# A recurrent attention and feed-forward block: one program block for four batches, masks behind the exp, stacks refilled by group

## The reference

```python
xn = layernorm(x)
q, k, v = xn @ Wq, xn @ Wk, xn @ Wv              # k, v repeated for two heads each
norm = |xn|;  mean = mean over tokens
score = 0.7 * norm + 0.3 * (-(xn . mean) / (norm * |mean| + 1e-6))
lm = top 337 tokens by score, dilated by 2       # landmarks
mask = (j <= i) & ((i - j < 128) | lm[j])
s = softmax(q k / 4 + where(mask, 0, -10000)) @ v @ Wo
g = silu(gelu(xn @ ternary(w1).T + b1) @ ternary(w2).T + b2)
out = x + s * g
```

## Time and profile before

| | |
|---|---|
| profiled execution | 737.96 us |
| its span, first to last instruction | 736.3 us |
| mean granted TensorE clock | 0.935 of 2.4 GHz |
| PE busy | 628.7 us, 85% |
| DVE busy | 375.4 us, 51% |
| ACT busy | 475.7 us, 65% |
| POOL busy | 74.7 us, 10% |
| scores, masks, values on PE (L718, L725, L738) | 198.5, 105.1, 167.4 us |
| exps on ACT (L812, L815) | 175.8, 204.9 us |

### The profile page before, as it was taken

The page is one execution under the profiler, slowest core; times in us unless marked ns, Lnnn a source line. Parts: engine busy times, 40 slices in busy tenths (PEclk is TensorE's granted clock), DMA queues, the critical chain, the costliest instruction groups (busy, mean ns, idle before and its releaser), DMA issues. The chain is left out here.

```text
span 736.3 us, 11753 instructions
## 1 busy us (share of the span) xinstructions
PE 628.7 (85%) x4336; PEld 351.7 (48%) x4336; DVE 375.4 (51%) x1002; ACT 475.7 (65%) x723; POOL 74.7 (10%) x92
## 2 busy tenths in 40 slices
PE   0537809999999989999999679999999899799982
PEld 0524604664455546654554536654554556334532
DVE  7968961665827434767454615648364521410101
ACT  1112417677877766697768556697768666888680
POOL 4000020020010201020100301110100210201001
PEclk9968957999999979999999869999999899899997
DMA  7000699000145659001190756001082691030101
GB/s 214 0 0 1 83 89 153 9 8 20 47 62 77 73 116 144 16 8 31 35 124 21 83 143 102 11 8 58 16 115 37 80 137 42 7 90 8 52 10 49
DMA packets 46833, 43.84 MB, mean 60 GB/s; under 512 B 6065, under 2 KB 41394, under 8 KB 46770
## 3 DMA queue, kind: packets, MB, share of 16 engines
q1 hardware_dynamic: 44642, 41.18, 33.6%
q10 hardware_dynamic: 2128, 1.84, 0.8%
HBM read 11.28 MB, written 4.19 MB: 21 GB/s over the span
## 5 line engine op out<-in xcount | busy, mean ns | idle before, releaser
L812 ACT ACTIVATE probs<-sc_ps,shift 128x512 f32<-128x512 f32 (+1 forms) x288 | 175.8, 617 | 102.0 <-PE sc_ps L725 101.3
L718 PE MATMUL sc_ps<-q_stack,k_stack 99*128 99x512 bf16 (+3 forms) x768 | 198.5, 344 | 33.3 <-PEq L189 14.7
L815 ACT ACTIVATE probs<-sc_ps,key_bias 128x1024 f32<-128x1024 f32 (+3 forms) x256 | 204.9, 818 | 16.5 <-PE sc_ps L718 15.8
L738 PE MATMUL att_ps<-probs,v_sb 128*32 128x512 f32 (+3 forms) x1536 | 167.4, 508 | 0.0
L718 PEld LDWEIGHTS sc_ps<-q_stack,k_stack 99*128 99x128 bf16 x768 | 50.2, 99 | 182.9 <-issue 70.8
L725 PE MATMUL sc_ps<-near_mask,mask_ident 128*128 128x256 bf16 (+1 forms) x576 | 105.1, 266 | 0.0
L850 POOL TENSOR_TENSOR h_lo<-hid,h_hi 128x512 fp32r<-128x512 f32 x32 | 43.2, 1350 | 342.3 <-DVE h_hi L882 342.3
L725 PEld LDWEIGHTS sc_ps<-near_mask,mask_ident 128*128 128x128 bf16 x576 | 56.4, 103 | 37.5 <-issue 7.1
L665 PE MATMUL aux_ps<-w2T,h_hi 128*128 128x256 f32 x256 | 70.1, 307 | 0.0
L665 PE MATMUL aux_ps<-w2T,h_lo 128*128 128x256 f32 x256 | 63.2, 279 | 0.0
L773 ACT ACTIVATE hid<-aux_ps,b_sb 128x512 f32<-128x512 f32 x64 | 42.9, 687 | 22.8 <-PE aux_ps L655 13.8
(11 more groups left out here) (152 smaller groups left out, 748.9 us busy)
## 6 DMA issues: line engine op xcount, KB each, us to landing
q_stack<-q_parts SPq DMA_DIRECT2D x96, 128.0 KB, 8.1
k_stack<-k_parts SPq DMA_DIRECT2D x24, 256.0 KB, 8.8
xn<-in_L_attn_hidden_states SPq DMA_DIRECT2D x4, 1024.0 KB, 8.2
attT<-att_raw SPq DMA_DIRECT2D x128, 32.0 KB
rden_bc<-den SPq DMA_DIRECT2D x64, 64.0 KB
probs<-in_L_ffn_w SPq DMA_DIRECT2D x2, 1024.0 KB, 7.8
out_y<-xn SPq DMA_DIRECT2D x4, 512.0 KB, 6.1
xn<-in_L_attn_hidden_states SPq DMA_DIRECT2D x3, 512.0 KB, 4.0
```

The lines of the kernel that those rows point to most:

```text
L718: last = pe.matmul(sc_ps[:, 2 * u + hh, lo:CH], k_stack[0:KROWS + SHIFT_ROWS, h // REP, kb * P:(kb + 1) * P], q_stack[0:KROWS + SHIFT_ROWS ...
L738: last = pe.matmul(att_ps[32 * q:32 * q + 32, n % 2, lo:CH], v_sb[:, kb, j * VW:j * VW + 32], probs[:, i % 3, q, lo:CH], start=(kb == 0), ...
L812: last = act.activation(probs[:, i % 3, us, lo:near], sc_ps[:, us, lo:near], ACT.Exp, bias=shift[:, 0:1], scale=HD ** -0.5)
L815: last = act.activation(probs[:, i % 3, us, near:CH], sc_ps[:, us, near:CH], ACT.Exp, bias=key_bias[:, kb:kb + 1], scale=HD ** -0.5)
```

## The change

The first blocks stay. Behind them the program now branches: the old turns are kept, for inputs with a large bound, as `general_path`, which these inputs do not take; the others take `fast_path`, a single block that is written out for all four batches (192 steps, numbered s; s % 48 is the old step number) with no barrier and no clearing between them. In it:

- **Masks.** `scores` has no mask matmuls and 96 rows in place of 99. `exps` makes one ACTIVATE for each u. Behind the exp POOL zeroes the upper triangle of the diagonal block (`causal`: a select on 128 x 4 x 128 numbers, in 32 steps of a batch), and DVE multiplies the next block by `near`, which is 1 within the window or for a landmark key (`local`: 128 x 4 x 128, in 28 steps). Queries beyond take `v_far`, a copy of V with the rows of all other keys zeroed, made once per batch in `commit`. So `values` of steps with both kinds (20 of a batch) have eight matmuls, on parts of the queries.
- **Values.** They are done for two steps together at each odd s, for s - 3 and s - 2, behind `scores(s, 1)`. At even s both halves of the scores stand together, ahead of the jobs; at odd s the jobs stand between the halves. `probs` has four buffers in place of three.
- **Stacks.** `q_stack` is a ring of three groups; each group has six DMAs of 64 KB (`fill_q`), issued when the group three before it has had its scores. `k_stack` is refilled for two key heads at a time (`fill_k`), when the last group that uses them is done. The columns of Wq and Wk are laid out by group for it.
- **Other.** The mean over tokens is summed on POOL (`token_sum`, seven additions of 128 x 256) and needs one matmul in place of eight. The squared norms of the tokens come from the layer norm's variance. x for the residual has a buffer of its own. The two clears of 32 rows of the stacks on DVE (L298, L299) are gone from the set-up. `ffn_up` of the next batch's chunk 0 stands at step 43.5 and `v_proj` at 42, where both came behind step 47. The table of the jobs' places has changed in small ways.

```diff
         exact = nc.values_load(exact_flag[0:1, 0:1], min_val=0, max_val=1)
-        turn(None, False, True, False, None)
-        turn(0, True, True, False, x[1])
-        with nc.Fori(1, B - 1) as b:
-            turn(b, True, True, True, x[b + 1])
-        turn(B - 1, True, False, True, None)
+        with nc.If(exact != 0):
+            general_path()
+        with nc.Else():
+            fast_path()
...
-                    def stack_q(c):
-
-                        cs = slice(c * CH, (c + 1) * CH)
-                        for i in range(NPART):
-                            for m in range(QT):
-                                sp.dma_start(q_stack[i * HD:(i + 1) * HD, m * HT:(m + 1) * HT, cs],
-                                             q_parts[:, m, QPART[i], cs]).then_inc(stack_in[c], 16)
...
+                        def fill_q(n):
+
+                            b, c, g = n // NG, n % NG // GROUPS, n % GROUPS
+                            m = g // QT
+                            if n >= QSLOTS:
+                                sp.wait_ge(sc_done, 2 * (GEND[n - QSLOTS] + 1))
+                            sp.wait_ge(q_split, QT * NC * b + QT * c + m + 1)
+                            for i in range(NPART):
+                                src = q_parts[half_rows(g), m, QPART[i], c * CH:(c + 1) * CH]
+                                sp.dma_start(q_stack[i * HD:(i + 1) * HD, n % QSLOTS, :, :], src).then_inc(q_in[n % QSLOTS], 16)
...
+                        def fill_k(b, g):
+                            if b:
+                                sp.wait_ge(sc_done, 2 * (GEND[(b - 1) * NG + GROUPS + g] + 1))
+                            sp.wait_ge(k_split, NC * (b + 1))
+                            for i in range(NPART):
+                                src = k_parts[g * 2 * HD:(g + 1) * 2 * HD, KPART[i], :]
+                                sp.dma_start(k_stack[i * HD:(i + 1) * HD, 2 * g:2 * g + 2, :], src).then_inc(k_in[g], 16)
...
-                                last = pe.matmul(sc_ps[:, 2 * u + hh, lo:near], mask_ident[:, :], near_mask[:, first:end:kb + 1, :],
-                                                 start=False, stop=True)
-                        last.then_inc(sc_done, 1)
...
+                        def exps(s, u):
+                            lo, _ = spans(s % NSTEP)
+                            if s >= NPROB and u == 0:
+                                act.wait_ge(pv_done, s - NPROB + 1)
                             us = slice(2 * u, 2 * u + 2)
-                            if near > lo:
-                                last = act.activation(probs[:, i % 3, us, lo:near], sc_ps[:, us, lo:near], ACT.Exp,
-                                                      bias=shift[:, 0:1], scale=HD ** -0.5)
-                            if near < CH:
-                                last = act.activation(probs[:, i % 3, us, near:CH], sc_ps[:, us, near:CH], ACT.Exp,
-                                                      bias=key_bias[:, kb:kb + 1], scale=HD ** -0.5)
-                            last.then_inc(exp_done, 1)
-
...
-                        lk(dve.tensor_scalar(near_mask[:, 0, :], before[:, :], MASK_UNIT, None, ALU.mult))
-                        for t in range(T - 1):
-                            last = dve.tensor_scalar(near_mask[:, t + 1, :], before[:, :], landmark[:, t:t + 1], -MASK_UNIT, ALU.max, ALU.mult)
-                        lk(last)
-                        dve.tensor_scalar(near_mask[:, 1:T, :], near_mask[:, 1:T, :], MASK_UNIT, None, ALU.add)
...
+                        def causal(s):
+                            c, _, kb = STEPS[s % NSTEP]
+                            own_q = slice((kb - TC * c) * P, (kb - TC * c + 1) * P)
+                            block_probs = probs[:, s % NPROB, :, own_q]
+                            pool.wait_ge(exp_done, 2 * (s + 1))
+                            pool.affine_select(out=block_probs, in_=block_probs, compare_op=ALU.is_ge, fill=0.0, base=0,
+                                               pattern=[[0, NQ], [1, P]], channel_multiplier=-1).then_inc(tri_done, 1)
...
+                        def commit(b):
+                            dve.wait_ge(v_done, 2 * (b + 1))
+                            if b:
+                                dve.wait_ge(pv_done, b * NSTEP - 2)
+                                dve.wait_ge(local_done, LOCALS[b * NSTEP - 1])
+                            for t in range(T - 1):
+                                dve.tensor_scalar(near[:, t, :], before[:, :], landmark[:, t:t + 1], None, ALU.max)
+                            dve.tensor_tensor(v_far[:, :, :], v_sb[:, b % 2], landmark[:, :].unsqueeze(2).to_broadcast([P, T, VP]),
+                                              ALU.mult).then_inc(far_done, 1)
+                            dve.wait_ge(far_done, b + 1)
+
+                        def local(s):
+                            c, _, kb = STEPS[s % NSTEP]
+                            nxt = slice((kb + 1 - TC * c) * P, (kb + 2 - TC * c) * P)
+                            block_probs = probs[:, s % NPROB, :, nxt]
+                            dve.wait_ge(exp_done, 2 * (s + 1))
+                            dve.tensor_tensor(block_probs, block_probs, near[:, kb, :].unsqueeze(1).to_broadcast([P, NQ, P]),
+                                              ALU.mult).then_inc(local_done, 1)
+
...
+                                pe.wait_ge(tri_done, TRIS[s])
+                            if has_local(s % NSTEP):
+                                pe.wait_ge(local_done, LOCALS[s])
+                            lo, end = spans(s % NSTEP)
+                            ends = [(v_sb[:, b % 2], lo, end), (v_far, end, CH)]
+                            for w, first, stop in ends:
+                                if first == stop:
+                                    continue
+                                for q in range(NQ):
+                                    j = (g * NQ + q) // REP
+                                    last = pe.matmul(att_ps[32 * q:32 * q + 32, n % 2, first:stop], w[:, kb, j * VW:j * VW + 32],
+                                                     probs[:, s % NPROB, q, first:stop], start=(kb == 0 and first == lo),
+                                                     stop=(kb == TC * (c + 1) - 1), skip_group_check=True)
...
-                                scores(i, 0)
-                            if i >= LAG:
-                                values(i - LAG)
-                            if i < NSTEP:
-                                scores(i, 1)
-                            for j in jobs_at(i, i + 0.5):
+                            if 0 <= s < TOTAL:
+                                scores(s, 0)
+                                if s % 2 == 0:
+                                    scores(s, 1)
...
+                            if 0 <= s < TOTAL and s % 2:
+                                scores(s, 1)
+                            if s % 2 and 3 <= s < TOTAL + 3:
+                                values(s - 3)
+                                values(s - 2)
...
+                        jobs += [(p + 16, "mean_row", b)]
+                        jobs += [(p + at, "transpose", b, n % KD, n // KD) for n, at in enumerate((19, 19, 20, 21))]
+                        jobs += [(p + 22 + c, "k_proj", b, c) for c in range(NC)]
+                        jobs += [(p + at, "q_proj", b, n % QT, n // QT) for n, at in enumerate((24, 26, 29, 31))]
+                        jobs += [(p + 30, "score_row", b, i) for i in range(2)]
+                        jobs += [(p + 41, "dilate", b)]
+                        jobs += [(p + 42, "v_proj", b, i) for i in range(2)]
+                        jobs += [(p + 43.5, "ffn_up", b, 0, f) for f in range(FT)]
...
+                    jobs += [(o + 10 + i, "ffn_down", b, i // 2, i % 2) for i in range(2 * TC)]
+                    jobs += [(o + 17.5, "ffn_up", b, 1, f) for f in range(FT)]
+                    jobs += [(o + 27 + t, "out_proj", b, t) for t in range(TC)]
+                    jobs += [(o + 34 + i, "ffn_down", b, TC + i // 2, i % 2) for i in range(2 * TC)]
+                    jobs += [(o + (57 + t // 2), "out_proj", b, TC + t) for t in range(TC)]
...
```

2108 lines of the change are left out of this document (1340 added, 768 removed).

## The result

The changed kernel takes 767.06 us (median of 4 runs, 765.11 to 773.68), the kernel before 737.26 in the same comparison: 1.0422 times as long, 95% interval 1.0351 to 1.0492. The forecast was 684, with a range of 656 to 718. It is slower by 30 us, where 54 us less were forecast.

What follows compares the result with a forecast made beforehand. PE's stream was taken as the bound in both chunks. 736.3 - 35.1 - 4.8 - 7.2 - 20.1 - 17.7 = 651.4; + 18 + 3 = 672.4; + 10 = 682.4, 684 us as device time; range 656 to 718.

Steps and rivals of the forecast that it cites:

- four chunks 0, with the boundary's wait: Chunk 0 of all four batches: 132.7 us against 167.8 before, plus 18 for waits at three boundaries.
- four chunks 1, with bursts and SILU: Chunk 1 of all batches: 322.9 us against 327.7; four bursts 7.2 less; boundary work 36.6 against 56.7.
- ranking 3, slip 10: Allowances: 3 us for products held back by DVE's bunched ranking, 10 us as 2% of 500 us.
- What is new on other engines: Select and product stay hidden, DVE has room for 28 products per batch; 3 us for ranking, 18 at boundaries.
- The boundary's wait: At each batch's step 9 PE waits 6 us at `out_proj` for heads behind DMAs; 3 x 6 = 18 us.
- Rival 2: PE's idle time in full pairs brings half clock, 2.7 us more per pair; chance 0.12, of which 0.08 slower.
- The pair order: A full pair of steps takes 5.19 us, PE's work only 3.57, leaving PE about 1.6 us idle for jobs.
- The split of the values: Values in two parts cost nothing more, the 0.15 counted once; otherwise 0.15 each on 80 steps, 12 us.
- Bursts: Four `ffn_up` bursts take 11 us instead of 12.8, as ACT starts its GELUs earlier: -7.2 us.
- The front: Set-up before the first exp: its place moves from 111.5 to about 93.8 us, -17.7; `lm_pad` about 94.
- mask matmuls cost PE in full: Mask matmuls on PE's stream: 6.2 us per batch in chunk 0, 7.0 in chunk 1, the latter mostly lost again.
- the detour's price of about nothing: Select on POOL and product on DVE, 1.6 us and two handovers, stay hidden within 2.7 us before the values.

Runs made afterwards that it cites:

- e13: Changed kernel with DVE's preparation jobs and chunk 0's `out_proj` at later places, `dilate` at step 46 behind the second burst: 746.9 us, 1.013 times the kernel before.
- e1: Changed kernel with the normalisation of chunk 0's heads at step 23 of DVE's list instead of 25: 757.1 us, 1.0305 times the kernel before.
- e9: Changed kernel with `out_proj` reading a tile of `xT_hi` instead of the normalised heads, attention left out of the output: 751.4 us, 1.0191 times the kernel before.
- e4: Changed kernel with 60 filler matmuls in front of the first `out_proj` of each chunk: 776.3 us, 1.0555 times the kernel before.
- e11: Changed kernel with DVE's preparation jobs and chunk 0's `out_proj` at later places, `dilate` at step 42: 772.4 us, 1.0471 times the kernel before.
- e10: Changed kernel without selects and products (masks missing), PE and ACT in the order of the kernel before: 735.1 us, 0.9973 times the kernel before.
- e7: Changed kernel without selects and products on the exp's results (masks missing), pair order kept: 757.1 us, 1.0274 times the kernel before.
- e2: Changed kernel with the single-step order of the kernel before on PE and ACT, masks kept: 785.2 us, 1.0642 times the kernel before.
- e8: Kernel before without the matmuls that add the masks to the scores: 696.4 us, 0.9438 times the kernel before.
- e6: Changed kernel with boundary list altered: x load behind the last sums, reciprocals, heads and layer norm later, all `out_proj` at step 58: 764.8 us, 1.0371 times before.
- e16: Changed kernel with e13's later places, single order with values of s - 3, and boundary reciprocals, heads and `out_proj` one step later: 733.3 us, 0.9961 times before.
- e17: e16 with the first batch's `dilate` at step 2 of PE's list instead of 0, near masks and two products behind it: 736.8 us, 0.9992 times before.

## Why the prediction was wrong

The terms, as the exps' starts give them, against the forecast (span 763.1 against 682.4, 80.7 us):

| term | forecast | measured | error |
|---|---|---|---|
| first exp's place | 93.8 | 92.9 | -0.9 |
| four chunks 0, with the boundary's wait | 150.7 | 175.0 | +24 |
| four chunks 1, with bursts and SILU | 403.5 | 473.3 | +70 |
| tail, as before | 21.4 | 21.9 | +0.5 |
| ranking 3, slip 10 | 13 | within the others | -13 |

**The step that failed** is "What is new on other engines", in the sentence on DVE's load: "That is room enough on the whole". It judged DVE by its busy share (58% now), with 3 us for the ranking. But PE doesn't wait for DVE's total; it waits for a certain place in DVE's list. I looked for such a meeting only at the boundary (step 9, 6 us), where the list was behind a DMA. The same meeting at step 27, where nothing but DVE's own work of steps 22 to 24 stood ahead, I did not look for: there 3 x 8.8 = 26 us. The experiments show it: the same operations at other places, 20 us less (e13); the wait taken from one job goes in part to the next in the list (e1, e9). These 26 us are a third of the 80.7. The other terms follow, of which the bursts weigh as much.

**The boundary's wait** had the right place and mechanism, and the wrong price. PE waited there 2.1 us for a product and 1.9 for the heads in batch 1, 2.5 and 2.4 in batch 2, and not at all in batch 3. The product stood behind the reciprocal, for which DVE waited:

```profile
275.73 0.94 DVE L1684 RECIPROCAL f_den<-f_den 64x128 f32<-64x128 f32 x1 [7.59 <-DMA f_den<-f_att_raw]
```

Steps 6 to 11 of batch 1 exceed the forecast's 13.6 without a wait by 11.0 us. The 7 beside the two waits go with the granted clock of 0.79; no run parts them further. The chain of DMAs itself was priced well: `den` landed 13.4 us after step 48's first exp (262.3; forecast 13.5), and L1689 ran at 283.65, 21.4 after it (forecast 22.5). But PE reached `out_proj` only 20.9 us after it, not 17.5, since it had lost time at the product before.

**The clock.** Rival 2 had half clock in the idle time of each full pair, for whole stretches. In chunk 1 that did not happen: steps 22 to 33 of batch 3, most of them without jobs, ran at 1.00. In chunk 0 it did happen in part. Steps 0 to 5 of batch 1 ran at 1.00 (the first row of the nine above), the same steps of batch 3 at 0.70, though no wait of PE in them was longer than 0.84 us. Here are these steps 0 to 5, then steps 22 to 33, of batch 3:

```profile
606.02:620.99 14.97, 11.69 (x90) 4.47 (x88) 7.85 (x14) 9.59 (x13) 5.69 (x6) 0.70 0.29 83
677.50:704.40 26.90, 22.55 (x201) 9.91 (x200) 8.46 (x12) 20.51 (x24) 9.46 (x10) 1.00 0.12 40
```

The same work took 3.3 us more. Why one batch and not the other, no run shows. The longer waits are plainer: from the first `dilate` to the last exp PE waited sixteen times for 1.88 us or more, and each time the granted clock fell to 1.2 GHz during the wait or within about 1 us of its end. That cost 3.5 us at step 27 (e4) and some 6 at `dilate` (e11). My slip of 2% has it far too small. Beside this stands the Trainium skill (TensorE: Matmul & The Clock Gate, "A second HAM failure mode: psum-queue depth-cycling"), which puts such falls down to short idle times between groups of matmuls; steps 0 to 5 of batch 3 fit that, those of batch 1, with waits up to 1.12 us, do not, and the costly falls here come with single waits of 2 to 10 us.

**The pair order** was priced right: 20/21 takes 4.95 us (5.10 forecast), 24/25 4.48 (4.13), 32/33 4.21 (4.13). What I had not seen is what it buys: a longer way from the exp to the values. I had it as a cost alone. It costs 22 us (e10 against e7), and while the product stands in DVE's list it saves that and 18 more (e2).

**The split of the values** priced at nothing is right. At full clock, the parts of steps 8 and 9:

```profile
296.29 0.64 PE L1392 MATMUL att_ps<-f_probs,f_v_sb 128*32 128x256 f32 x8
296.75 0.62 PE L1392 MATMUL att_ps<-f_probs,f_v_far 128*32 128x256 f32 x8
297.18 0.61 PE L1392 MATMUL att_ps<-f_probs,f_v_sb 128*32 128x256 f32 x8
297.61 0.40 PE L1392 MATMUL att_ps<-f_probs,f_v_far 128*32 128x128 f32 x8
```

to 297.95 are 1.66 us, where unsplit 512 and 384 queries would be 1.64 by my formula with the 0.15 counted once, as forecast, and 1.79 with it counted twice.

**Bursts** of 11 us: I took 1.8 off without a row for it. The burst and its two pairs' share came to 18.8 and 21.6 instead of 15.4 and 20.2, in three batches 3 x 4.8 = 14 us. In all seven bursts PE ends its part early and then waits for the exp, which stands on ACT behind the GELUs, two table loads and the SILU: 4.9 us each time, as long as the wait at step 27. The first burst of batch 1 now, and the same place in turn 0 of the kernel before:

```profile
327.47 1.03 PE L1369 MATMUL sc_ps<-f_q_stack,f_k_stack 96*128 96x512 bf16 x2 [4.95 <-ACT f_probs L1473]
...
159.87 3.62 PE L697 MATMUL aux_ps<-xn,ones 128*128 128x256 f32 x16
163.33 1.34 PE L679 MATMUL aux_ps<-ident,xn 128*128 128x128 f32 x8
```

Before, the mean over tokens (3.62) and transposes filled that time. The change moved the mean to POOL and the transposes behind the wait, so that part of what it took from PE had cost nothing. Behind the wait the clock falls, and the pairs after the bursts take 7.2 to 8.1 us (18/19) and 6.3 to 7.2 (44/45) where the forecast has 5.2 and 5.1, at a granted clock of 0.57 to 0.74: some 15 us in all that it did not have. In turn 3 of the kernel before, where nothing is prepared, PE waits 4.24 us at that place and the next 12 us have a clock of 0.72; in turn 0 they have 1.00. No run fills this wait in the changed kernel, so this term is argued, not shown.

**The front** came where forecast (92.9), but `lm_pad` did not (101.5, forecast 94). DVE's ranking now stands on both sides of the burst's 8.9 us without a gap. It began at 76.7, 2.6 us sooner than before, and took 25.0 us with the burst's splits, where it took 22.0: so the gain of the set-up was gone before `dilate`. PE stood at `dilate` for 10.5 us, and the first pair took 11.4 where 2.5 of wait were said to be hidden: 7.5 us.

**Masks.** That mask matmuls cost PE in full was right for three quarters (41 of 53, e8), and the detour's price of about nothing was 10 (e7).

Against the kernel before, by batches from first exp to first exp: 15, 8, 16 and 6 us longer, 1 in the tail, less 19 at the front: the 27 us between the spans. How the 39 us divide that lie between e10 (735) and the old kernel without masks (696) is only half settled: about 20 are the places in the lists (e13, measured in the pair order with masks); the rest I did not part. Steps 8 to 11 take 21 to 23 us in batches 1 to 3 of e10, where the forecast has 10 and 6 of wait, and e6, e16 and e17 did not remove what stands at the boundary and at the first `dilate`.

## What to carry to other kernels

When a change puts work on an engine with a free half, don't add up its time: write down, for each result that the bounding engine waits for, what stands ahead of it in the other engine's list, waits for DMAs included, and what stands behind it in the waiting engine's. Price such a wait at more than its length, as the clock falls with it: here 4.95 us cost 8.8 at step 27 and 2.94 cost 9.2 at `dilate`, where much of PE's work stood behind. Before you take work away from the bounding engine, look at what would stand in its place: a wait that the work had filled comes to light. And don't judge an order of issue apart from the latency that it hides: the same reordering was worth +18 and -22 us.
